# Two staging tiles for the moved queries, and SyncE's other transfers spread over the pairs of heads

## The reference

```python
mod = (silu(c) @ wmod).reshape(8, 6, 1, 256)          # sa, ca, ga, sb, cb, gb
h = layernorm(x) * (1 + ca) + sa
x = x + ga * attention(h)
h = layernorm(x) * (1 + cb) + sb
x = x + gb * (experts(h) + shared(h))

# attention: 16 heads, causal over 512 tokens
kv  = h @ w_kv_a                      # 192 for the queries, 64 latent keys, 64 rotary keys
q   = rmsnorm(kv_q) @ w_qb            # per head 128 plain + 64 rotary
scores = (q_nope . k_nope + q_pe . k_pe) / sqrt(192)
attn = softmax(scores) @ v;  out = attn @ w_o
# experts: softmax over 16, top 4, at most 128 tokens an expert
```

## Time and profile before

| | |
|---|---|
| Median of 3 runs | 1278.34 us (1276.54 to 1278.9) |
| The profiled execution | 1274.24 us, of which the trace's span is 1272.0 |
| PE busy | 1141.7 us (90%) |
| VectorE, ScalarE, GpSimd busy | 781.3 (61%), 624.8 (49%), 479.5 us (38%) |
| Mean granted TensorE clock | 0.965 of 2.4 GHz |
| SyncE's DMA queue | 98.56 MB, its packets 32.0% of the time of 16 engines |

### The profile page before, as it was taken

How to read it: one execution, slowest core, us unless ns; L and a number is a source line. 1 busy time by engine, 2 the same in 40 slices (tenths; PEclk the granted TensorE clock), 3 DMA queues, 4 the chain that set the end, 5 groups by cost and what they waited for, 6 DMA issues and landing times.

```text
span 1272.0 us, 23491 instructions
## 1 busy us (share of the span) xinstructions
PE 1141.7 (90%) x6444; PEld 865.9 (68%) x6444; DVE 781.3 (61%) x2404; ACT 624.8 (49%) x1840; POOL 479.5 (38%) x524
## 2 busy tenths in 40 slices
PE   5698998999989998999989998999989999898693
PEld 3576776777667766777667766777667767776462
DVE  3566656665766567665767567665767568664541
ACT  2256634665356634655356534555356535563120
POOL 1222115450445324450445324450445325442364
PEclk8799999999999999999989999999989999999897
DMA  9352205540353205440353105340353205530793
GB/s 303 94 131 67 68 5 141 105 100 1 82 134 86 47 17 138 95 99 1 83 133 90 43 18 137 94 99 1 83 133 87 46 17 137 96 83 1 211 248 40
DMA packets 87555, 114.34 MB, mean 90 GB/s; under 512 B 16346, under 2 KB 51096, under 8 KB 87456
## 3 DMA queue, kind: packets, MB, share of 16 engines
q1 hardware_dynamic: 68416, 98.56, 32.0%
q0 software_dynamic: 7168, 6.20, 2.5%
q10 hardware_dynamic: 11872, 8.65, 2.5%
HBM read 35.56 MB, written 15.11 MB: 40 GB/s over the span
## 4 chain that ended last, share of the span: by engine, by line
PE 39%; DVE 13%; issue 12%; DMA 11%; SPq 10%; ACT 8%; POOL 4%; ACTq 2%; DVEq 1%; POOLq 0%
DMA qT<-qstage 9%; SPq L445 9%; PE PS L805 6%; PE PS L784 4%; ACT probs L1136 4%; PE PS L963 3%; PE PS L942 3%; PE PS L934 3%; PE PS L763 2%; PE PS L765 2%; PE PS L764 2%; DVE pT L1401 2%; PE PS L913 2%; PE PS L915 2%; POOL tab_dram L621 1%
## 5 line engine op out<-in xcount | busy, mean ns | idle before, releaser
L1136 ACT ACTIVATE probs<-probs,nmax 128x512 f32<-128x512 f32 (+3 forms) x512 | 282.8, 554 | 195.6 <-DVE nmax L1387 192.8
L1387 DVE CUSTOM_DVE_ANT_0 probs<-PS,cmask 128x512 f32<-128x512 f32 (+3 forms) x512 | 231.0, 488 | 119.6 <-PE PS L765 92.2
L763 PE MATMUL PS<-kTh,qT 128*128 128x512 f32 (+3 forms) x512 | 182.2, 356 | 27.0 <-DVE nmax L1387 21.8
L784 PE MATMUL PS<-ident,probs 128*128 128x128 f32 x1280 | 167.0, 278 | 26.9 <-ACT pT L1145 16.5
L784 PEld LDWEIGHTS PS<-ident,probs 128*128 128x128 f32 x1280 | 139.3, 141 | 49.6 <-ACT pT L1145 22.9
L559 POOL TENSOR_TENSOR qr<-qr 128x512 f32<-128x512 f32 x64 | 81.5, 1274 | 236.1 <-DVE qr L1373 235.9
L764 PE MATMUL PS<-kTl,qT 128*128 128x512 f32 (+3 forms) x512 | 167.4, 327 | 0.0
L765 PE MATMUL PS<-kTh,qT 128*128 128x512 f32 (+3 forms) x512 | 167.3, 327 | 0.0
L805 PE MATMUL PS<-pT,kmat 128*64 128x512 f32 (+3 forms) x1024 | 162.4, 462 | 0.3 <-issue 0.3
L1145 ACT ACTIVATE pT<-PS 128x384 f32<-128x384 f32 (+3 forms) x320 | 124.3, 449 | 42.0 <-PE PS L784 42.0
L763 PEld LDWEIGHTS PS<-kTh,qT 128*128 128x128 f32 x512 | 98.5, 192 | 47.4 <-DVE nmax L1387 24.0
(11 more groups left out here) (254 smaller groups left out, 1867.9 us busy)
## 6 DMA issues: line engine op xcount, KB each, us to landing
qT<-qstage SPq DMA_DIRECT2D x128, 256.0 KB, 3.5
qT<-qstage SPq DMA_DIRECT2D x256, 128.0 KB, 3.5
x_in<-in_x SPq DMA_DIRECT2D x8, 512.0 KB, 11.9
modb<-mod_dram SPq DMA_DIRECT2D x8, 512.0 KB, 5.6
h_dram<-mod_dram SPq DMA_DIRECT2D x8, 512.0 KB, 11.6
h_dram<-h SPq DMA_DIRECT2D x8, 512.0 KB, 3.4
out<-base SPq DMA_DIRECT2D x8, 512.0 KB, 4.2
pT<-in_wo SPq DMA_DIRECT2D x1, 2048.0 KB, 11.3
```

Of the source, the lines that this page charges most:

```text
L763: pe.matmul(PS[:, bank, 0:n], qh, kTh[:, 0:n], start=True, stop=False)
L784: mm = pe.transpose(PS[:, bank, col:col + P], probs[:, UO[u] + j * P:UO[u] + (j + 1) * P], ident[:])
L1136: act.activation(probs[:, UO[u]:UO[u] + UW[u]], probs[:, UO[u]:UO[u] + UW[u]], ACT.Exp, scale=-1.0, bias=nmax[:, u:u + 1], accum_out=psums ...
L1387: dve.tensor_tensor_reduce(out=probs[:, UO[u]:UO[u] + UW[u]], in0=PS[:, SBANK[u], 0:UW[u]], in1=cmask[:, S - UW[u]:S], scale=-1.0, scalar= ...
```

## The change

Four things are changed.

1. `qstage` becomes two tiles, used by pairs of even and odd number in turn. `latent_high(p)` waits for the move of pair p-2 in place of p-1; the first use of the second tile, `latent_high(0, 1)`, waits for none. `ql1t`, which borrows plane 3 for a moment in `middle`, borrows it from the second tile.
2. SyncE's other transfers stand one behind each move: x of the batch after next behind move 2, the store of `base` behind move 3, `modb` behind move 4, the gate rows behind move 5 (of batch 7 behind all moves). Its loop runs six times and the seventh pass is written out. Three waits are made by `wait_alone`, which computes the value ahead of the wait.
3. On GpSimd `shared` goes from behind the rotary work of pair 2 to behind that of pair 3.
4. `h2T` is another name for `hT`, `chosen` another for `ohs`.

```diff
-        h2T = sb("h2T", [P, 2, S])
+        h2T = hT
...
-        qstage = sb("qstage", [P, 4, S], F32R)
+        qstage = [sb(f"qstage{k}", [P, 4, S], F32R) for k in range(2)]
...
-        chosen = sb("chosen", [P, NT * TOPK, NE])
+        chosen = ohs[:].rearrange("p t k e -> p (t k) e")
...
-                src = qstage[frm:frm + n, 2 * hl:2 * hl + 2, :].bitcast(F32)
+                src = qstage[p % 2][frm:frm + n, 2 * hl:2 * hl + 2, :].bitcast(F32)
...
-            for p in range(3):
-                move_query(0, p, p < 2)
-            gate_rows(0)
-            with sp.Fori(0, B - 1) as b:
-                n = b + 1
-                sp.wait_ge(h1_ready, n)
-                sp.wait_ge(res_ready, n)
+            def load_x(n):
+                wait_alone(sp, h1_ready, n)
+                wait_alone(sp, res_ready, n)
                 sp.dma_start(x_in[:], rows(xr, n)).then_inc(x_landed, 16)
-                for p in range(3, NPAIR):
+
+            def batch(b, n, more):
+                for p in range(5, NPAIR):
                     move_query(b, p)
+                    if p == 5:
+                        gate_rows(b)
                 for p in range(2):
                     move_query(n, p)
                 store_rows(b)
                 move_query(n, 2)
+                if more:
+                    load_x(n + 1)
+                move_query(n, 3)
                 store_batch(b)
+                move_query(n, 4)
                 load_modb(n)
-                gate_rows(n)
-            for p in range(3, NPAIR):
+
+            for p in range(5):
+                move_query(0, p, p < 2)
+                if p == 2:
+                    load_x(1)
+            with sp.Fori(0, B - 2) as b:
+                batch(b, b + 1, True)
+            batch(B - 2, LAST, False)
+            for p in range(5, NPAIR):
                 move_query(LAST, p)
+            gate_rows(LAST)
...
-                query_rotary(n * NPAIR + 2, n * NPAIR)
-                shared(b)
+                query_rotary(n * NPAIR + 2, 0, n * NPAIR)
                 for p in range(1, NPAIR - 2):
-                    query_rotary(n * NPAIR + p + 2, n * NPAIR + p)
+                    query_rotary(n * NPAIR + p + 2, p % 2, n * NPAIR + p)
+                    if p == 1:
+                        shared(b)
                     scatter(b, p)
...
-                    act.wait_ge(q_landed[(p + 1) % 2], landed(b, p - 1) if p else landed(b - 1, NPAIR - 1))
-                act.activation(qstage[:, 0, :], PS[:, LATBANK, :], ACT.Copy).then_inc(lath_ready, 1)
+                    act.wait_ge(q_landed[p % 2], landed(b, p - 2) if p >= 2 else landed(b - 1, p + NPAIR - 2))
+                act.activation(qstage[p % 2][:, 0, :], PS[:, LATBANK, :], ACT.Copy).then_inc(lath_ready, 1)
...
-                    latent_high(n, 1)
+                    latent_high(n, 1, not post)
```

More of the change, by code:

```diff
@@ L172, in adaln_block @@
         qr = sb("qr", [P, 2, S])
-        qstage = sb("qstage", [P, 4, S], F32R)
+        qstage = [sb(f"qstage{k}", [P, 4, S], F32R) for k in range(2)]
         qT = [sb(f"qT{k}", [P, 2, 2, S], F32R) for k in range(2)]
-        ql1t = qstage[:, 3, :]
+        ql1t = qstage[1][:, 3, :]
         probs = sb("probs", [P, sum(UW)])
@@ L460, in store_batch @@
             def store_batch(b):
-                sp.wait_ge(base_ready, b + 2)
+                wait_alone(sp, base_ready, b + 2)
                 sp.dma_start(rows(outr, b), base[:]).then_inc(base_out, 16)
@@ L554, in widen, with query_rotary @@
                                      [P, 2, NT, KL])).then_inc(wide_ready, 1)
-            def query_rotary(g, w=None):
+            def query_rotary(g, slot, w=None):
                 wait_alone(pool, turned_ready, g + 1)
@@ L562, in query_rotary @@
                 wait_alone(pool, peh_ready, g + 1)
-                pool.tensor_tensor(qstage[:, 3, :], qr[:, 0, :], qstage[:, 2, :].bitcast(F32),
+                pool.tensor_tensor(qstage[slot][:, 3, :], qr[:, 0, :], qstage[slot][:, 2, :].bitcast(F32),
                                    ALU.subtract).then_inc(pel_ready, 1)
@@ L629, in between @@
                 roots_post(b)
-                query_rotary(n * NPAIR)
+                query_rotary(n * NPAIR, 0)
                 rows_scaled(b)
-                query_rotary(n * NPAIR + 1)
+                query_rotary(n * NPAIR + 1, 1)
                 rows_shifted(b, n)
                 counts(b, False)
-                query_rotary(n * NPAIR + 2, n * NPAIR)
-                shared(b)
+                query_rotary(n * NPAIR + 2, 0, n * NPAIR)
                 for p in range(1, NPAIR - 2):
-                    query_rotary(n * NPAIR + p + 2, n * NPAIR + p)
+                    query_rotary(n * NPAIR + p + 2, p % 2, n * NPAIR + p)
+                    if p == 1:
+                        shared(b)
                     scatter(b, p)
@@ L647, in _ @@
             for p in range(NPAIR):
-                query_rotary(p, p - 2 if p >= 2 else None)
+                query_rotary(p, p % 2, p - 2 if p >= 2 else None)
             root_h1(1)
@@ L1125, in latent_high @@
                 if not fresh:
-                    act.wait_ge(q_landed[(p + 1) % 2], landed(b, p - 1) if p else landed(b - 1, NPAIR - 1))
-                act.activation(qstage[:, 0, :], PS[:, LATBANK, :], ACT.Copy).then_inc(lath_ready, 1)
+                    act.wait_ge(q_landed[p % 2], landed(b, p - 2) if p >= 2 else landed(b - 1, p + NPAIR - 2))
+                act.activation(qstage[p % 2][:, 0, :], PS[:, LATBANK, :], ACT.Copy).then_inc(lath_ready, 1)
             def rotary_high(b, p):
                 act.wait_ge(rope_ready, b * NPAIR + p + 1)
-                act.activation(qstage[:, 2, :], qr[:, 0, :], ACT.Copy).then_inc(peh_ready, 1)
+                act.activation(qstage[p % 2][:, 2, :], qr[:, 0, :], ACT.Copy).then_inc(peh_ready, 1)
             def exps(g, units):
@@ L1375, in q_rope, with q_low @@
                 return [first, lambda: swapped(0, KL), lambda: swapped(KL, 0).then_inc(turned_ready, 1)]
-            def q_low(g):
+            def q_low(g, slot):
                 dve.wait_ge(lath_ready, g + 1)
-                dve.tensor_tensor(qstage[:, 1, :], PS[:, LATBANK, :], qstage[:, 0, :].bitcast(F32),
+                dve.tensor_tensor(qstage[slot][:, 1, :], PS[:, LATBANK, :], qstage[slot][:, 0, :].bitcast(F32),
                                   ALU.subtract).then_inc(latl_ready, 1)
@@ L1434, in step @@
                 if rope:
-                    q_low(g + 2)
+                    q_low(g + 2, p % 2)
                 if more and p in (NPAIR - 4, NPAIR - 3):
@@ L1486, in last_seats @@
                 ch.step(dve.tensor_scalar(taken[:], rank, 1.0, None, ALU.add))
-                ch.step(dve.tensor_tensor(chosen[:].rearrange("p (t k) e -> p t k e", k=TOPK), oh[:],
+                ch.step(dve.tensor_tensor(chosen.rearrange("p (t k) e -> p t k e", k=TOPK), oh[:],
                                           taken[:].unsqueeze(2).to_broadcast([P, NT, TOPK, NE]), ALU.mult))
-                ch.step(dve.tensor_reduce(seatk[:], chosen[:], AX.X, ALU.add))
+                ch.step(dve.tensor_reduce(seatk[:], chosen, AX.X, ALU.add))
                 for t in range(NT):
@@ L1628, in middle @@
                         part()
-                    q_low(n * NPAIR)
+                    q_low(n * NPAIR, 0)
                 if not post:
@@ L1649, in middle @@
                 if pre:
-                    q_low(n * NPAIR + 1)
+                    q_low(n * NPAIR + 1, 1)
                 if post:
```

2 lines of the change are left out of this document (1 added, 1 removed).

## The result

The changed kernel takes 1227.6 us (median of 4 runs, 1226.56 to 1229.8), the kernel before on the same chip 1277.44. The ratio is 0.9615, 95% interval 0.9592 to 0.9638. The profiled execution took 1228.22 us, 46.0 less than the profiled one before.

What follows compares the result with a forecast made beforehand. The loop through the one query staging tile was taken to bound the pair step; 40.9 us gained less 1.5 off 1274.24 gives 1234.8, plus 4.1 for timed runs 1239 us; range 1231 to 1257.

Steps and rivals of the forecast that it cites:

- the price of moving `shared`: GpSimd's `shared` behind pair 3 fits with 0.8 us to spare: taken as 0, at most 2.4 us lost, seven times.
- the 4.1 us added for the timed runs: Timed runs' median 1278.34 us stood 4.1 above the profiled execution, so 1234.8 became 1239 us.
- gate rows: On SyncE's queue, gate rows issued behind move 5 may delay move 6 at seven places: 1.5 us lost in all.
- step 6 to 7: Where `h1_normed` interrupts VectorE, no wait for the move occurs: counted nothing, bounds 0 to 4 us gained.
- steps 2 to 6: Two staging tiles bring these pair steps down to 11.15 us each, in all batches: 40.9 us gained.
- The new wait is never the last one: ScalarE's `latent_high(p)` waits for pair p-2's move, already seen landed by PE; its 107.9 us of waits go.
- 11.15 as PE's own step: Distance between first value matmuls in a pair step where PE waits for nothing: 11.15 us, against 12.17 in batch 4.
- Rival B: Gate rows hold up move 6 by 2.9 us at seven places, 20 us: 1259 us; chance 0.10.
- One tile for `hT` and `h2T`, `chosen` on `ohs`: Sharing these tiles adds no wait, as PE's reads come earlier in its order: 0.
- A: PE's own step is 11.65 us, so only its idle time at L784, 23.0 us, comes back: 1255; chance 0.18.
- D: No change: another loop of 12.2 us takes over, such as the move's issue and landing; 1278 us, chance 0.05.
- C: Each spread transfer delays the next move, 1.3 us past the slack at PE's scores, 40 times: 1290 us; chance 0.05.

Runs made afterwards that it cites:

- e5: Changed kernel with a second, equal copy of each batch's gate rows issued by SyncE right behind the first, in batches 0 to 6; 1279.27 us.
- e8: Changed kernel with a second copy of the gate rows in batches 0 to 6, issued from ScalarE's queue instead of SyncE's; 1275.05 us.
- e3: Changed kernel with only GpSimd's `shared` back in its old place, behind pair 2; 1238.42 us.
- e7: Changed kernel with `shared` back behind pair 2 and VectorE's 64 slot numbers kept in PSUM instead of SBUF; 1229.13 us.
- e1: Changed kernel with SyncE's transfers in the old order and `shared` in its old place, so the staging tiles alone; 1237.81 us.
- e2: Kernel before, still with one staging tile, given SyncE's new order and `shared` behind pair 3; 1259.47 us.
- e10: Changed kernel with an extra copy on ScalarE's queue of 512 different rows of x, instead of one row read 512 times; 1228.03 us.
- e6: Changed kernel with VectorE's batch loop written out seven times instead of run as a loop; 1197.73 us.

## Why the prediction was right, and where it was wrong

The forecast of 1239 us is 11.4 above the measured 1227.6. The case was right: faster, by the staging tiles, with the other moves of work at little cost. The step that failed is the price of moving `shared`: the prediction put it at nothing, and it measured -5.8 us. A second term, the 4.1 us added for the timed runs, was no property of the kernel and accounts for another 4.7. These two make 10.5 of the 11.4 us. Either of them put right alone, with the range moved along, would have taken in the result (a low end of 1225.2 or 1226.9). The other terms cancel by luck: 3.3 us too much gain for the tiles against 3.4 too little for the gate rows and step 6 to 7; 0.8 are left at the start and the end. Term by term (first pair of profiled executions, the second pair in brackets):

| | predicted | measured |
|---|---|---|
| steps 2 to 6 | -40.9 | -37.6 (-36.7) |
| gate rows | +1.5 | 0 |
| step 6 to 7 | 0 (gain up to 4) | -1.9 (-1.9) |
| `shared`, in the middles | 0 | -5.8 (-5.9) |
| start, steps 1 to 2, end | 0 | -0.8 (-2.7) |
| profiled to timed runs | +4.1 | -0.6 (-1.8) |

- **Staging tiles.** "The new wait is never the last one" held, and so did 11.15 as PE's own step (11.17 in batches 0 to 6). The term is 3.3 us too large because one batch stood for six: batch 1 was at 47.36 us before, not 48.66, and the step in which VectorE takes the statistics of x is 11.25 and not 11.15.
- **Gate rows.** A wait for move 6 occurs nowhere, and the slack is the 2.5 us worked out. But the late landing was taken from a row that does not match. In batch 7 of before the gate rows were not alone ahead of the move: the output and `modb` went out just before them, and the move behind all three landed 16.3 us after the gate rows' issue.

```profile
1074.11 0.41 SPq L462 DMA_DIRECT2D out<-base  x1
...
1074.71 0.40 SPq L435 DMA_DIRECT2D modb<-mod_dram  x1
```

  With the gate rows alone ahead of it, move 6 is through 13.6 us after their issue (521.36 to 535). The step's first value matmul starts at 521.45, so this is no later than the 13.5 us behind it that the prediction had for a move with nothing ahead. The gate rows' packets of 1 KB end 9.0 us after the issue in batch 3, and 8.5 to 10.8 in the others, while SyncE is already issuing move 6. Rival B was nearer than its chance says: e5 shows that one more copy of them costs the whole gain. The Trainium skill's rule that the prediction weighed (page "DMA: Bandwidth & Descriptors", section "Queues, rings and completion order"), that each engine consumes descriptors in ring order, agrees with e5, where the move's last DMA landed 10.84 us after its issue, and with e8. The length of the wait came from the repeated source row, of which neither the rule nor rows 6 and 7 tell.
- **`shared`: the step that failed.** The prediction asked only whether `shared` fits in its new place, and bounded it by a loss of 2.4 us. "I take 0" left out what it did in its old place: there it held up VectorE's addition by 0.7 us in all seven middles. In six of them, those with the loop branch behind, this stood on the way to PE's next scores; the seventh hardly changed (51.95 and 51.87 us). Both rows were in the trace of before (they stand in the section on the result, at 640.56 and 642.09). e3 and e7 show it by putting it back and by taking the conflict away alone. Of the 0.97 us in each of the six, 0.73 is the operation. The stop behind the branch is also 0.2 to 0.3 us shorter without the conflict (3.7 to 3.8 us before, 3.4 to 3.7 after, 3.4 to 3.5 in e7); what sets that is not traced.
- **"On that scale."** The prediction added 4.1 us because the profiled execution of before was that much below the median of three runs. The changed kernel's was 0.6 above its median. The distance of one execution from a median is chance: the 17 runs of the kernel before that were taken beside e1 to e5 have a median of 1276.55, 2.3 above its profiled execution. Without these 4.1 us the forecast would have been 1234.8.
- **One tile for `hT` and `h2T`, `chosen` on `ohs`.** No run takes these out by themselves. e2 keeps the tiles apart, and its middles (384.7) are 1.0 to 1.1 us below those of the changed kernel, so a cost can hardly be larger than that.
- **Rivals.** A (11.65 a step) and D are refuted by 11.17; C by the missing waits ahead of pairs 3 to 7.

## What to carry to other kernels

When an operation is moved, price what it did to its neighbours in the old place as well as in the new: look there for an operation of another engine that lasts longer than its size explains and ends when the moved one ends. Predict from one execution to one execution, and give the scatter of the timed runs to the range, not to the forecast. The two tiles were right because one loop (copy, move, landing, next copy) was as long as the step; after it was gone, the next two limits were a loop branch (28 to 30 us in the timed runs) and an order of work (10 us), both visible in the same trace as short waits that come once a batch.

## What the runs showed of the hardware

- A VectorE addition of two SBUF tiles took 0.95 us instead of 0.23 while a GpSimd operation on SBUF ran, and 0.23 beside it with one input in PSUM (e3, e7).
- A DMA that reads one 1 KB row of DRAM 512 times ran at 45 to 65 KB a us in the stretches shown, whether one queue or two did so; 512 rows of x took 2 us, some 250 KB a us (e5, e8, e10).
- VectorE's taken loop branch stopped it for 3.4 to 3.9 us in every kernel with the loop; behind the idle time of PE that follows, its granted clock was 0.54 over 7 us, and both went with the loop (e6).
